# A cross-attention layer on one core: two passes over the scores in one software pipeline, straight code instead of loops

## The chip, the cores and the metric

One core of a Trainium2 chip. The time is device microseconds for one execution of the whole program. Engines: PE is TensorE, ACT ScalarE, DVE VectorE, POOL GpSimd, SP the queue that issues every DMA of this kernel.

## The reference

For B = 8 batches of S = 256 tokens, D = 1024 features, 32 heads of 32 features, all in f32:

```python
x = (hidden - mu) * rsqrt(var + 1e-5) * ln_gamma + ln_beta     # layer norm over 1024
Q = split_heads(x @ Wq.T)
K = V = split_heads(ctx)                                        # [8, 256, 1024]
scores = einsum('bhsd,bhtd->bhst', Q, K) / sqrt(32)             # masked with -inf
probs = softmax(scores)
attn = einsum('bhst,bhtd->bhsd', probs, V)
return hidden + merge_heads(attn) @ Wout.T
```

## The kernel before

**Numbers as pairs of f16.** Weights, normalised x, context, q and attention output are kept as a high and a low f16 part. A product takes three matmuls (`PASSES`). The high part is a copy by ACT, the low part (value minus high part) an operation of DVE; each such pair of operations on a 128x512 PSUM tile is a "fill" or "split" (`wq_split`, `wo_split`, `z_split`, `k_split`, `q_split`; z is the normalised x, transposed).

**Two passes over the scores.** Softmax needs the log of the sum of exponentials (lse) for each query row, and the probabilities are wanted with keys on partitions. So every batch has 16 steps of a first pass (`scores_s`, L399: four matmuls into a four-bank score buffer; `max_step`, L700: two maxima by DVE; `row_sums`, L554: four exps by ACT with an accumulated sum), and 16 steps of a second pass (`scores_t`, L426: four matmuls with the lse rows stacked in; `exp_step`, L572: one exp of 128x1024 by ACT; `probs_times_v`, L440, once for two steps; `att_split` by ACT and DVE). lse goes half a batch at a time: `ln_sums`, `exp_ln` on ACT, `lse_half` on DVE, two transposes on PE (`l_transposes`), `lse_rows` on DVE (five operations), three DMAs into row 97 to 99 of `q_stack`.

**Buffers.** Two score buffers `score[0]`, `score[1]` (four PSUM banks together of the eight, 2 banks each) are used alternately by both passes; `pv[0..1]` and `mm[0..1]` are one bank each. Step n waits for the reader of step n-2.

**Order of a batch.** `iteration(b)` writes the order of every engine by hand. First the 16 steps of the first pass of batch b, among which PE does the transposes of z and of the context of batch b+1 and the 96 output matmuls of batch b-1 (`o_matmuls`, L378); then the 16 steps of the second pass, among which it does nearly all 192 q matmuls of batch b+1 (`q_matmuls`, L354). DVE does row statistics, the Newton steps for 1/sqrt(var) and the normalising of batch b+2 in the second pass. POOL multiplies by gamma and adds beta, broadcast to all partitions, before the transposes (`scale_and_shift`, L284).

**Loops.** PE runs batches 1 to 6 in `pe.Fori(1, B - 1, 2)` (L514), two batches to a turn, three turns; ACT, DVE, SP and POOL have loops of their own (L628, L830, L262, L293).

**DMAs.** `fill_k_stack` and `fill_q_stack` copy the parts of k and q from 128 partitions to stacks of 32-partition groups: 12 DMAs each and a 13th for the mask, issued by SP in one order with all loads and stores (`iteration`, L190).

## Time and profile before

| | us |
|---|---|
| median of three runs | 649.28 |
| lowest, highest | 645.79, 653.34 |
| the profiled execution, in all | 647.76 |
| its span, first to last instruction | 646.0 |
| mean granted clock of TensorE, share of full | 0.976 |

How the profile is read: a row of the timeline has the start in us from the span's start, the length in us, the engine, the line of the kernel, the operation, what it writes and reads with its shape, the number of instructions merged into the row, and in brackets how long the engine sat idle before it and what ended the wait. "issue" there is a wait for nothing that the profile shows. Rows of groups give the count, total busy time and mean ns of one, and the idle time before them. The second number of a group of matmuls in the timeline includes a tail after the last, so that neighbouring groups overlap a little.

### The profile page before, as it was taken

The page shows a single profiled execution, that of the slowest core. Times are in us where ns is not written, and L with a number is a line of the kernel's source. Part 1 is how long each engine was busy: PE and PEld are TensorE (multiplying, and loading weights), DVE is VectorE, ACT ScalarE, POOL GpSimd, SP SyncE. Part 2 cuts the span into 40 slices and gives each one's busy share as a digit, 9 for nine tenths or more (in the row PEclk, how much of TensorE's full clock was granted, in tenths as well). Part 3 has the DMA queues.
Part 4 walks back from the last instruction along what each step waited for, and adds up shares of the span by engine and source line. Part 5 has one row for each costly group of instructions (what it writes and reads, how often), then busy time and mean ns, then how long its engine had stood idle before and what let it go on. Part 6 is the DMA issues. An engine that isn't in the chain of part 4 may idle for free.

```text
span 646.0 us, 13668 instructions
## 1 busy us (share of the span) xinstructions
PE 586.4 (91%) x4768; PEld 394.7 (61%) x4768; DVE 378.4 (59%) x813; ACT 457.5 (71%) x1377; POOL 80.8 (13%) x38
## 2 busy tenths in 40 slices
PE   3688688999999999689999999969999999998897
PEld 3587466656776577455776567635676558744443
DVE  6856686478545865258654876238763793168311
ACT  2633898798768976469767986639866996689850
POOL 2406000600060003200032000500015000000000
PEclk9999699999999999979999999969999999999999
DMA  8787122434344243413335162331523431422203
GB/s 329 273 211 195 43 70 66 116 115 116 106 117 128 82 117 106 133 29 90 108 110 136 53 164 64 91 114 50 149 63 91 133 110 36 117 50 66 69 2 98
DMA packets 37020, 69.67 MB, mean 108 GB/s; under 512 B 8833, under 2 KB 10081, under 8 KB 36962
## 3 DMA queue, kind: packets, MB, share of 16 engines
q1 hardware_dynamic: 36962, 68.84, 36.9%
q8 instruction: 44, 0.72, 0.5%
q14 instruction: 14, 0.11, 0.1%
HBM read 34.61 MB, written 8.39 MB: 67 GB/s over the span
## 4 chain that ended last, share of the span: by engine, by line
PE 65%; DVE 10%; ACT 10%; issue 6%; DMA 4%; SPq 4%; DVEq 0%
PE mm L369 20%; PE mm L394 17%; PE pv L448 10%; PE score L436 9%; ACT score L560 8%; PE score L412 6%; DVE nmax L706 4%; SPq L152 2%; PE pv L334 2%; DMA x_nat<-in_x 2%; DVE o_buf L748 1%; PE pv L349 1%; ACT probs L577 1%; SPq L171 1%; DMA probs<-in_L_xattn_Wq 1%
## 5 line engine op out<-in xcount | busy, mean ns | idle before, releaser
L560 ACT ACTIVATE score<-score,nmax 128x256 f32<-128x256 f32 x512 | 232.5, 475 | 16.0 <-DVE nmax L706 15.3
L706 DVE TENSOR_REDUCE nmax<-score 128x2 f32<-128x512 f32 x256 | 164.0, 685 | 66.3 <-PE score L412 65.8
L394 PE MATMUL mm<-woT,aT 128*128 128x512 f16 x768 | 186.6, 384 | 1.5 <-DVE o_buf L748 1.5
L369 PE MATMUL mm<-zT,wqT 128*128 128x256 f16 x1536 | 185.2, 274 | 2.0 <-DVE zT L657 2.0
L577 ACT ACTIVATE probs<-score 128x1024 f32<-128x1024 f32 x128 | 124.0, 1024 | 71.7 <-PE score L436 71.4
L369 PEld LDWEIGHTS mm<-zT,wqT 128*128 128x128 f16 x1536 | 150.1, 98 | 23.5 <-issue 2.9
L394 PEld LDWEIGHTS mm<-woT,aT 128*128 128x128 f16 x768 | 75.5, 98 | 74.8 <-DVE o_buf L748 4.4
L560 ACT ACTIVATION_READ_ACCUMULATOR score<-score,nmax 128x1 f32 x512 | 119.6, 234 | 0.0
L412 PE MATMUL score<-k_stack,q_stack 97*128 97x256 f16 x512 | 81.0, 281 | 31.0 <-issue 14.1
L287 POOL TENSOR_TENSOR x_nat<-x_nat,gamma_b 128x1024 f32<-128x1024 f32 x16 | 41.7, 2605 | 409.9 <-DVE x_nat L697 409.9
L741 DVE TENSOR_TENSOR aT<-pv,aT 128x256 f16<-128x256 f32 x64 | 27.0, 424 | 112.6 <-ACT aT L583 111.8
L412 PEld LDWEIGHTS score<-k_stack,q_stack 97*128 97x128 f16 x512 | 47.9, 100 | 68.7 <-ACT score L560 27.0
L436 PE MATMUL score<-q_stack,k_stack 100*128 100x256 f16 x512 | 67.8, 274 | 2.9 <-ACT probs L577 1.1
L448 PE MATMUL pv<-probs,ctx_sb 128*32 128x256 f32 x1024 | 68.5, 385 | 0.9 <-DVE aT L741 0.6
L436 PEld LDWEIGHTS score<-q_stack,k_stack 100*128 100x128 f16 x512 | 45.4, 98 | 29.7 <-issue 18.5
L448 PEld LDWEIGHTS pv<-probs,ctx_sb 128*32 128x32 f32 x1024 | 27.3, 109 | 25.5 <-issue 13.6
L546 ACT ACTIVATE zT<-pv 128x512 f16<-128x512 f32 x32 | 19.3, 605 | 27.8 <-PE pv L334 27.8
L289 POOL TENSOR_TENSOR x_nat<-x_nat,beta_b 128x1024 f32<-128x1024 f32 x16 | 38.8, 2424 | 1.3
L748 DVE SCALAR_TENSOR_TENSOR o_buf<-mm,res 128x512 f32<-128x512 f32 x32 | 21.8, 681 | 17.3 <-PE mm L394 17.3
L583 ACT ACTIVATE aT<-pv 128x256 f16<-128x256 f32 x64 | 24.9, 393 | 8.5 <-PE pv L448 8.5
L662 DVE SCALAR_TENSOR_TENSOR qT<-mm,qT 128x512 f16<-128x512 f32 x32 | 22.1, 690 | 14.6 <-ACT qT L552 14.1
L552 ACT ACTIVATE qT<-mm 128x512 f16<-128x512 f32 x32 | 19.6, 611 | 14.8 <-PE mm L369 14.8
(46 smaller groups left out, 322.7 us busy)
## 6 DMA issues: line engine op xcount, KB each, us to landing
k_stack<-kT SPq DMA_DIRECT2D x192, 64.0 KB, 2.0
q_stack<-qT SPq DMA_DIRECT2D x192, 64.0 KB, 2.4
x_nat<-in_x SPq DMA_DIRECT2D x8, 1024.0 KB, 5.3
ctx_sb<-in_ctx SPq DMA_DIRECT2D x8, 1024.0 KB, 6.3
res<-in_x SPq DMA_DIRECT2D x32, 256.0 KB, 3.5
out<-o_buf SPq DMA_DIRECT2D x32, 256.0 KB, 2.5
probs<-in_L_xattn_Wq SPq DMA_DIRECT2D x8, 512.0 KB, 7.3
probs<-in_L_xattn_Wout SPq DMA_DIRECT2D x8, 512.0 KB, 6.4
```

The lines of the kernel that those rows point to most:

```text
L287: pool.tensor_tensor(x_nat[:, st], x_nat[:, st], gamma_b[:], ALU.mult).then_inc(gamma_done, 1)
L289: pool.tensor_tensor(x_nat[:, st], x_nat[:, st], beta_b[:], ALU.add).then_inc(z_done, 1)
L369: last = pe.matmul(mm[i % 2][:, m2 * S:(m2 + 1) * S], wqT[:, wp, k, m * P:(m + 1) * P], zT[:, zp, k, :], start=(v2 == 0), stop=(v2 == KT * ...
L394: last = pe.matmul(mm[i % 2][:], aT[:, ap, k, st * P:(st + 1) * P], woT[:, wp, k, nh * 512:(nh + 1) * 512], start=(v == 0), stop=(v == O_M ...
L412: last = pe.matmul(score[n % 2][:, j, :], q_stack[0:S_ROWS, h, j, gl, st * P:(st + 1) * P], k_stack[0:S_ROWS, pb, h, j, gl, :], start=True ...
L436: last = pe.matmul(score[n % 2][:, j, :], k_stack[0:T_ROWS, pb, h, j, gl, tt * P:(tt + 1) * P], q_stack[0:T_ROWS, h, j, gl, :], start=True ...
L448: last = pe.matmul(pv[g % 2][DH * j:DH * (j + 1), 0, :], ctx_sb[:, pb, tt, g * P + DH * j:g * P + DH * (j + 1)], probs[:, g % 2, tt, j, :] ...
L560: last = act.activation(score[n % 2][:, j, :], score[n % 2][:, j, :], ACT.Exp, bias=nmax[:, st, h, j, gl:gl + 1], accum_out=sums[:, st, h, ...
L577: act.activation(probs[:, g % 2, tt], score[n % 2][:], ACT.Exp).then_inc(exp_done, 1)
L706: dve.tensor_reduce(nmax[:, st, h, at, gl], score[n % 2][:, at, :], AX.X, ALU.max, negate=True).then_inc(max_done, 1)
L741: dve.tensor_tensor(aT[:, 1, g, :], pv[g % 2][:, 0, :], aT[:, 0, g, :], ALU.subtract).then_inc(a_lo, 1)
L748: dve.scalar_tensor_tensor(out=o_buf[:, i % 2, :], in0=mm[i % 2][:], scalar=1.0 / W_SCALE, in1=res[:, i % 2, :], op0=ALU.mult, op1=ALU.add ...
```

## The change

The kernel is reordered as a whole.

- **One pipeline of slots.** Every engine runs `slot(b, t)` for t = 0 to 15. A slot has step t of the second pass of batch b, and the step of the first pass that lies 12 steps further on (`LEAD = 12`, `first_step`): of batch b for t < 4, of batch b+1 from t = 4. Twelve slots of "batch -1" with no second pass come first, and among them are the transposes and splits of Wout.
- **PSUM.** `score_s` for the first pass and `score_t` for the second, one each of two banks; one bank each for `pv`, `tr` (all transposes), `mo` (output) and `mq` (q). Where there were two buffers of a kind there is one.
- **Matmuls dealt out.** `Q_TAIL`, `Q_HEAD` and `O_AT` give each slot its q matmuls (12 or 16, none in two slots) and output matmuls (5, 6 or 9).
- **gamma and beta behind the transposes.** They are loaded as 16 rows of 128, transposed once, and applied by DVE per partition when it copies the transposed tile from PSUM to `t_f32` (`z_scale`, two operations; `k_scale`, one). POOL then makes the high and the low f16 part (`z_split`, `k_split`: a copy and a subtract of 128x512); for the first batch ACT makes the high part. ACT has no z and k copies afterwards.
- **Buffers in SBUF.** `q_stack` and `aT` double, `probs`, `qT`, `kT` half; the context is loaded twice, once for the transposes (`c_nat`) and in halves for the second product (`v_nat`). The residual is loaded into `o_buf` (a ring of three) and added in place.
- **`probs_times_v`** is called for each step, not for two.
- **The last batch's output** uses four PSUM banks, with no wait between its tiles.
- **Start.** Order of loads and of work changed: z of batch 0 first, q tiles between the transposes of Wq.
- **No loops.** Every engine's code is written out.

The core of the diff, the buffers and what a slot is dealt first:

```diff
-        score = [es.enter_context(nc.psum_tensor(f"score{i}", [P, J, S], F32)) for i in range(2)]
-        pv = [es.enter_context(nc.psum_tensor(f"pv{i}", [P, 2, S], F32)) for i in range(2)]
-        mm = [es.enter_context(nc.psum_tensor(f"mm{i}", [P, 512], F32)) for i in range(2)]
+        score_s = es.enter_context(nc.psum_tensor("score_s", [P, J, S], F32))
+        score_t = es.enter_context(nc.psum_tensor("score_t", [P, J, S], F32))
+        pv = es.enter_context(nc.psum_tensor("pv", [P, 2, S], F32))
+        tr = es.enter_context(nc.psum_tensor("tr", [P, 2, S], F32))
+        mo = es.enter_context(nc.psum_tensor("mo", [P, 2, S], F32))
+        mq = es.enter_context(nc.psum_tensor("mq", [P, 2, S], F32))
...
+Q_TAIL = [108 + 12 * min(t, 7) for t in range(STEPS + 1)]
+Q_HEAD = [0] * 10 + [16, 32, 48, 64, 80, 96, 108]
+O_AT = [0, 6, 12, 18, 24, 29, 34, 39, 48, 57, 62, 67, 72, 77, 82, 87, 96]
+Q_ENDS = {2: (1, 2), 6: (1, 3), 11: (2, 0), 14: (2, 1)}
```

PE's waits of the two passes, and its slot:

```diff
+            def scores_s(b, n):
...
-                if n >= 2:
-                    pe.wait_ge(sum_done, b * STEPS + n - 1)
+                    pe.wait_ge(sum_done, b * STEPS + n)
...
+            def scores_t(b, n):
...
-                    pe.wait_ge(exp_done, b * STEPS + n - 1)
+                if b or n:
+                    pe.wait_ge(exp_done, b * STEPS + n)
...
+            def slot(b, t):
+                s_b, s_n = first_step(b, t)
+                if b >= 0:
+                    scores_t(b, t)
+                if t and b >= 0:
+                    probs_times_v(b, t - 1)
+                elif b >= 1:
+                    probs_times_v(b - 1, STEPS - 1)
+                if b < 0:
+                    wo_transposes(WO_AT[t])
+                if t == 5 and b >= 0:
+                    l_transposes(b, 1, 8 * min(b + 2, B))
+                if b + 2 < B:
+                    if t == 6:
+                        k_transposes(b + 2, 0, 2 * b + 2)
+                    if t == 7:
+                        z_transposes(b + 2, 0, 2 * b + 2)
...
+                if b + 1 < B:
+                    q_matmuls(b + 1, Q_TAIL[t], Q_TAIL[t + 1])
+                if b + 2 < B:
+                    q_matmuls(b + 2, Q_HEAD[t], Q_HEAD[t + 1])
+                if s_b < B:
+                    scores_s(s_b, s_n)
...
+                if b >= 1:
+                    at = O_AT_LAST if b == B - 1 else O_AT
+                    o_matmuls(b - 1, at[t], at[t + 1])
```

ACT's slot:

```diff
+            def slot(b, t):
+                s_b, s_n = first_step(b, t)
+                if b < 0:
+                    wo_split(WO_AT[t])
+                else:
+                    exp_step(b, t)
+                if t and t % 2 == 0 and b >= 0:
+                    att_split(b, t // 2 - 1)
...
+                if t in Q_ENDS and b + Q_ENDS[t][0] < B:
+                    ahead, i = Q_ENDS[t]
+                    q_split(b + ahead, i)
+                if s_b < B:
+                    row_sums(s_b, s_n)
```

DVE's slot:

```diff
+            def slot(b, t):
...
+                if t in (4, 8, 12) and b >= 1:
+                    add_residual(b - 1, t // 4 - 1, mo[:])
...
+                    if t == 7:
+                        z_scale(b + 2, 0)
...
+                if t and t % 2 == 0 and b >= 0:
+                    att_split(b, t // 2 - 1)
...
+                if t == 5 and b >= 0:
+                    lse_rows(b, 1)
+                if t == 13 and b + 1 < B:
+                    lse_rows(b + 1, 0)
+                if 0 <= b < B - 2:
+                    if t < 2:
+                        row_stats(b + 2, t)
+                    if t == 2:
+                        row_var(b + 2)
+                    if t in (2, 3, 4):
+                        row_rstd(b + 2, t - 2)
+                    if t in (5, 6):
+                        normalise(b + 2, t - 5)
+                if s_b < B:
+                    max_step(s_b, s_n)
...
+                if t == 4 and b >= 0:
+                    lse_half(b, 1)
```

POOL's split of a fill, and how every engine runs through the slots:

```diff
+            def z_split(a, i):
+                f = z_fill(a, i)
+                pool.wait_ge(f32_done, f + 1)
+                if i == 0:
+                    pool.wait_ge(q_ready, a * TILES)
+                at = slice(2 * i, 2 * i + 2)
+                pool.tensor_copy(zT[:, 0, at], t_f32[:, f % 2]).then_inc(split_hi, 1)
+                pool.wait_ge(split_hi, z_split_at(a, i))
+                pool.tensor_tensor(zT[:, 1, at], t_f32[:, f % 2], zT[:, 0, at], ALU.subtract).then_inc(split_done, 1)
...
+            for b in range(-1, B):
+                for t in range(PRE if b < 0 else 0, STEPS):
+                    slot(b, t)
```

## Rows read from the trace of the kernel before

**Rows 1.** Page, busy time, share of the span and instructions of each engine.

```profile
PE 586.4 (91%) x4768; PEld 394.7 (61%) x4768; DVE 378.4 (59%) x813; ACT 457.5 (71%) x1377; POOL 80.8 (13%) x38
```

**Rows 2.** Timeline of PE: where batches begin, the loop's return, the last matmuls.

```profile
64.04 0.60 PE L412 MATMUL score<-k_stack,q_stack 97*128 97x256 f16 x4 [1.69 <-DMA q_stack<-qT]
...
128.99 0.61 PE L412 MATMUL score<-k_stack,q_stack 97*128 97x256 f16 x4
...
198.89 0.61 PE L412 MATMUL score<-k_stack,q_stack 97*128 97x256 f16 x4
...
267.79 1.07 PE L448 MATMUL pv<-probs,ctx_sb 128*32 128x256 f32 x16
...
276.25 0.82 PE L412 MATMUL score<-k_stack,q_stack 97*128 97x256 f16 x3 [4.03 <-issue]
...
568.59 0.61 PE L412 MATMUL score<-k_stack,q_stack 97*128 97x256 f16 x4
...
625.08 17.66 PE L394 MATMUL mm<-woT,aT 128*128 128x512 f16 x81
```

**Rows 3.** Timeline of PE: groups of one kind in a row.

```profile
58.49 2.78 PE L369 MATMUL mm<-zT,wqT 128*128 128x256 f16 x24
61.25 1.09 PE L317 MATMUL pv<-ident,probs 128*128 128x128 f32 x8
...
107.50 1.07 PE L448 MATMUL pv<-probs,ctx_sb 128*32 128x256 f32 x16
108.50 1.05 PE L436 MATMUL score<-q_stack,k_stack 100*128 100x256 f16 x8
```

**Rows 4.** Timeline: scores to maximum, maximum to row sums, the last of four.

```profile
90.50 0.61 PE L412 MATMUL score<-k_stack,q_stack 97*128 97x256 f16 x4 [0.94 <-ACT score L560]
...
91.15 1.29 DVE L706 TENSOR_REDUCE nmax<-score 128x2 f32<-128x512 f32 x2
...
225.26 1.28 DVE L706 TENSOR_REDUCE nmax<-score 128x2 f32<-128x512 f32 x2
...
225.98 0.45 ACT L560 ACTIVATE score<-score,nmax 128x256 f32<-128x256 f32 x1 [0.36 <-DVE nmax L706]
...
227.71 0.21 ACT L560 ACTIVATION_READ_ACCUMULATOR score<-score,nmax 128x1 f32 x1
```

**Rows 5.** Groups by line: att copy, att split and row statistics (busy, mean ns).

```profile
L583 ACT ACTIVATE aT<-pv 128x256 f16<-128x256 f32 x64 | 24.9, 393 | 8.5 <-PE pv L448 8.5
L741 DVE TENSOR_TENSOR aT<-pv,aT 128x256 f16<-128x256 f32 x64 | 27.0, 424 | 112.6 <-ACT aT L583 111.8
L669 DVE BATCH_NORM_STATS2 stats<-x_nat 128x6 f32<-128x512 f32 x32 | 19.7, 670 | 6.6 <-DMA x_nat<-in_x 6.6
```

**Rows 6.** Timeline of ACT and DVE: exps, Wout's fills, the first layer norm.

```profile
8.32 0.28 DVE L676 BATCH_NORM_AGGREGATE mean_var<-stats 128x2 f32<-128x12 f32 x2
...
11.63 1.53 DVE L697 TENSOR_SCALAR x_nat<-x_nat,mean_var,rstd 128x1024 f32<-128x1024 f32 x2
...
33.79 1.09 ACT L533 ACTIVATE woT<-pv 128x512 f16<-128x512 f32 x2 [2.46 <-PE pv L317]
34.42 1.29 DVE L646 SCALAR_TENSOR_TENSOR woT<-pv,woT 128x512 f16<-128x512 f32 x2 [2.37 <-ACT woT L533]
...
103.77 3.76 ACT L577 ACTIVATE probs<-score 128x1024 f32<-128x1024 f32 x4
```

**Rows 7.** Timeline: five operations of the lse rows to their DMAs; twelve DMAs of q.

```profile
104.99 0.41 DVE L729 TENSOR_SCALAR l_rows<-pv 16x256 f16<-16x256 f32 x1 [0.39 <-PE pv L423]
...
106.94 1.64 SPq L177 DMA_DIRECT2D q_stack<-l_rows  x2
...
119.95 7.49 SPq L171 DMA_DIRECT2D q_stack<-qT  x12
```

**Rows 8.** One line's instructions: POOL's add of beta, min/median/max ns.

```profile
L289 POOL TENSOR_TENSOR x_nat<-x_nat,beta_b x16: 2352/2358/3422, 15.5 to 490.4; 128x1024 f32<-128x1024 f32 x16
```

**Rows 9.** Page, DMA issues: count, KB each, median us to landing.

```profile
q_stack<-qT SPq DMA_DIRECT2D x192, 64.0 KB, 2.4
```

More of the change, by code:

```diff
@@ L387, in o_matmuls @@
[L387 to L395 removed]
+                        pe.wait_ge(a_lo, c * G + G - 1)
@@ L430, in scores_t @@
                     pe.wait_ge(l_in[h], (b + 1) * L_ROWS * DMA)
-                if n < 2:
-                    pe.wait_ge(sum_done, b * STEPS + STEPS - 1 + n)
-                else:
-                    pe.wait_ge(exp_done, b * STEPS + n - 1)
+                if b or n:
+                    pe.wait_ge(exp_done, b * STEPS + n)
                 for j in range(J):
-                    last = pe.matmul(score[n % 2][:, j, :], k_stack[0:T_ROWS, pb, h, j, gl, tt * P:(tt + 1) * P], q_stack[0:T_ROWS, h, j, gl, :],
+                    last = pe.matmul(score_t[:, j, :], k_stack[0:T_ROWS, b % 2, h, j, gl, tt * P:(tt + 1) * P], q_stack[0:T_ROWS, b % 2, h, j, gl, :],
@@ new lines, in probs_times_v @@
+            def probs_times_v(b, n):
+                g, tt = n // 2, n % 2
+                h, gl = divmod(g, HALF)
+                pe.wait_ge(exp_done, b * STEPS + n + 1)
+                if n in (0, STEPS // 2):
+                    pe.wait_ge(v_in[h], (b + 1) * DMA)
+                if b == 0 and n == 0:
+                    pe.wait_ge(wo_lo, W_FILLS)
+                elif tt == 0:
+                    pe.wait_ge(a_lo, b * G + g)
+                for j in range(J):
+                    at = gl * P + DH * j
+                    last = pe.matmul(pv[DH * j:DH * (j + 1), 0, :], v_nat[:, h, tt, at:at + DH], probs[:, n % 2, j, :],
+                                     start=(tt == 0), stop=(tt == ST - 1), skip_group_check=True)
+                last.then_inc(pv_done, 1)
@@ new lines, in _ @@
+            for f in range(4):
+                wq_split(f)
+            for i in range(TILES):
+                act.wait_ge(f32_done, i + 1)
+                act.activation(zT[:, 0, 2 * i:2 * i + 2], t_f32[:, i % 2], ACT.Copy).then_inc(z0_hi, 1)
+            for f in range(4, 8):
+                wq_split(f)
+            q_split(0, 0)
+            for f in range(8, 12):
+                wq_split(f)
+            q_split(0, 1)
+            for f in range(12, 16):
+                wq_split(f)
+            q_split(0, 2)
@@ L632, in _ @@
+            for b in range(-1, B):
+                for t in range(PRE if b < 0 else 0, STEPS):
+                    slot(b, t)
+            att_split(B - 1, G - 1)
         @block.vector
@@ L655, in z_split, with z_scale @@
-            def z_split(a, i):
-                dve.wait_ge(z_hi, a * FILLS + i + 1)
-                dve.tensor_tensor(zT[:, 1, 2 * i:2 * i + 2, :], pv[i % 2][:], zT[:, 0, 2 * i:2 * i + 2, :], ALU.subtract).then_inc(z_lo, 1)
+            def z_scale(a, i):
+                f = z_fill(a, i)
+                dve.wait_ge(fill_ready, f + 1)
+                if a == 0 and i >= 2:
+                    dve.wait_ge(z0_lo, i - 1)
+                elif a:
+                    dve.wait_ge(split_done, f - TILES - 1)
+                for m in range(2):
+                    k = 2 * i + m
+                    last = dve.tensor_scalar(t_f32[:, f % 2, m, :], tr[:, m, :], gb[:, 0, k:k + 1], gb[:, 1, k:k + 1], ALU.mult, ALU.add)
+                last.then_inc(f32_done, 1)
@@ L830, in _ @@
[L830 to L835 removed]
+            layer_norm(0)
+            dve.wait_ge(gb_ready, 1)
+            dve.tensor_copy(gb[:].rearrange("p a k -> p (a k)"), tr[:, 0, 0:2 * KT]).then_inc(gb_done, 1)
+            dve.wait_ge(gb_done, 1)
+            for i in range(TILES):
+                z_scale(0, i)
@@ new lines, in _ @@
+            for f in range(8):
+                wq_split(f)
+            dve.wait_ge(mask_in, DMA)
+            dve.tensor_scalar(mask_st, mask_u8, -1.0, 3e38, ALU.add, ALU.mult).then_inc(mask_ok, 1)
+            q_split(0, 0)
+            for f in range(8, 12):
+                wq_split(f)
+            q_split(0, 1)
+            for f in range(12, 16):
+                wq_split(f)
+            k_scale(0, 0)
+            k_scale(0, 1)
+            q_split(0, 2)
+            k_scale(0, 2)
+            k_scale(0, 3)
@@ L839 @@
+            layer_norm(1)
+            for b in range(-1, B):
+                for t in range(PRE if b < 0 else 0, STEPS):
+                    slot(b, t)
+            add_residual(B - 2, 3, mo[:])
+            att_split(B - 1, G - 1)
+            for i in range(TILES):
+                add_residual(B - 1, i, o_bank_last[i])
 _INS = ["x", "ctx_4096", "mask_BxS2_bf1", "L0_xattn_Wq", "L0_xattn_Wout", "L0_xattn_ln_gamma", "L0_xattn_ln_beta"]
```

891 lines of the change are left out of this document (399 added, 492 removed).

## The prediction

> **What bounds the kernel now.** I read the page's busy line first: PE is busy 91% of the span, ACT 71%, DVE 59%, POOL 13% [rows 1]. PE is the engine to follow, so I read its timeline for where one batch begins. Batch 1 starts its first-pass scores at 128.99, batch 2 at 198.89: 69.90 us. Batch 7 starts at 568.59, so six batches took 439.60, where six of 69.90 would be 419.40. The missing 20.2 us stand in one kind of place [rows 2]: after 267.79 (last product of batch 2, about 1.0 long) PE issues nothing useful until 276.25, with "issue" as releaser, and it is the return of `pe.Fori`. The clock is then down for some microseconds. There are two returns, 10.1 us each. The entry at 128.99 and the exit at 568.59 show no such gap.
>
> The pitches of PE's work [rows 3], from one row's start to the next's or, where another follows, less the tail of 0.17 by which a group's busy time overlaps the next: a q matmul 0.115 (24 in 61.25 - 58.49 = 2.76), a transpose 0.115 (8 in 1.09 - 0.17), a pv record 0.0625 (16 in 1.00), a score matmul 0.11 (8 in 1.05 - 0.17), and an output matmul 0.216 (81 in 17.66 - 0.17 [rows 2]). A batch has 192 q (22.1), 96 output (20.7), 64 + 64 scores (14.1), 128 pv records (8.0), 36 transposes (4.1): 69.0 us. So outside the loop's return the kernel before is within 1 us of PE's own work. **The change cannot gain more than about 1 us in a steady batch**; its possible gains are the 20.2 of the loop, batch 0 (65 us from 64.04 to 128.99 [rows 2], with about 49 of work) and the start.
>
> The Trainium skill (Runtime: NRT & Kernel Launch, section Instruction fetch mechanics) says that prefetch is sequential and a taken branch to code outside the window makes the engine wait for a fetch; the rows of the return agree, and straight code would by that rule give these microseconds back.
>
> **The new chain.** The change moves nothing off PE (the same matmuls and transposes, plus one small transpose). What it changes is who waits. Before, both passes alternate over two score buffers. After, the first pass has one buffer `score_s`, the second one `score_t`, and a slot does on ACT: exp of the second pass, att copy (even slots), a q copy (four slots), then the row sums of the first pass. On DVE the att split and other work stand ahead of `max_step`. The scores of slot t+1 may only start when the row sums of slot t are done. The price of that loop [rows 4]: scores start to max start 0.65 (90.50 to 91.15), max start to first row-sum exp 0.72 (225.26 to 225.98), four row sums to the end of the last accumulator read 1.94 (225.98 to 227.71 + 0.2), and 0.05 to PE. That is **3.36 us**, for odd slots with nothing else. In an even slot ACT must first do exp 0.94 (four in 3.76 [rows 6]) and the att copy 0.39, then DVE the att split 0.425, all of it ahead of the max [rows 5]: 0.94 + 0.39 + 0.05 + 0.425 + 0.05 + 0.72 + 1.94 = **4.51 us**. PE's mean slot is 69.0 / 16 = 4.3 us. A pair of slots is 7.9 by the chain and 8.6 by PE, so the bare pipeline is bound by PE with 0.7 to spare in a pair. But DVE's work for batch b+2 is put into the same slots ahead of the max:
>
> - t=0: two bn_stats, 1.3 [rows 5]. Slot 5.8.
> - t=2: variance and first Newton round. The 17 small instructions run 3.31 in all [rows 6], 9 of them 1.7. Slot 6.2.
> - t=4: Newton, 0.8. Slot 5.3.
> - t=5: `lse_half` ends after the max of slot 4, its transpose follows, then `lse_rows` 1.95 [rows 7] and a normalise of 0.77 [rows 6], then the max. Slot 5.1.
> - t=6: normalise again, 0.77. Slot 5.3.
> - t=7, 8: scaling of the transposed x, 0.84 a pair from PSUM by the att split's row, twice in each slot. Its splits are on POOL.
>
> **POOL.** The trace has no POOL copy and no 512-column subtract. A two-input add of 1024 columns takes 2.35 to 3.42, median 2.36 [rows 8], so 512 columns are 1.2; the copy lies between nothing and that 1.2. A fill then costs 1.2 to 2.4, and 3.4 if it runs like the slowest row; I take 2.1, because the copy has one input but its own start. Six fills come in slots 6 to 8, through one bank `tr`, two buffers `t_f32` and DVE's order; the chain k0, k1, z0..z3 ends about 10 us after the row sums of slot 6, and the q matmuls of slot 9 wait for it. They would otherwise start about 7.5 us after. So **2 to 3 us** of stall.
>
> The Trainium skill (GPSIMD Engine Reference, section 4.1) advises VectorE for elementwise work and gives two-input operations on GPSIMD as about 2x slower. No row here compares the two on one shape. By its figure of 2.6 cycles for an element a 512-column subtract would be 1.1 us; the sum would hardly move by that.
>
> Walking slot by slot, each the later of PE and chain, lateness carried on: stalls of 1.0 (t=0 to 1), 1.5 (2 to 3), 1.4 (4 to 5, with the wait of the lse transpose), 1.5 (6, 7), 2 (9), 0.3 (q bank, single, freed by ACT and DVE 2.7 after the last matmul while PE comes back after 2.2). A steady batch becomes 69 + 7 to 8 = **76 us**, against 69.9.
>
> **The sum.**
> - Start to first scores: norm is done at 13.2 [rows 6]; four z fills at 2.2 (transpose, scale, ACT copy, POOL subtract) to 22; q tiles 0 and 1 (5.5 each) with the wq fills between, whose DVE splits are serial behind them, to 39.4; k scale to 41.5; two POOL fills to 44. Only then SP issues the 13 DMAs of k_stack, and the 12 of q_stack behind them in its queue, at 0.625 each (12 in 7.49 [rows 7]): 15.6, and 2.4 to land [rows 9]. First scores at **62**, against 64.04, with q tile 3 and all but a fill of the wo transposes still to do.
> - Twelve leading slots: ACT wo copy 0.55 and DVE wo split 0.64 (pairs in 1.09 and 1.29 [rows 6]) stand ahead of each max: 4.0 a slot; two to a slot, the fills of batch 1 and lse bring **56**.
> - Batch 0, no output matmuls, by the chain: eight even and eight odd slots 63, DVE's extras and POOL 9: **72**.
> - Batches 1 to 5: 5 x 76 = **380**. Batch 6, no fills, chain 63 + 2: **65**. Batch 7: four slots of 3.9, twelve of 2.4 on PE: **45**.
> - Tail: 0.5 + 96 x 0.216 = 20.7 and 3.3 from PE's end to the last store (625.08 + 17.66 = 642.74 of 646.0 [rows 2]): **24.5**.
> Sum 704.5 on the span. The profiled run before is 646.0 on the span and 647.76 in all; the median is 649.28, so add 2 to 3. Some of the steps overlap at the joints (fills that slip into batch 0's idle PE), 5 us off: I forecast **702 us**, 8% slower. Where the 20.2 of the loop go: they are gained on PE and spent in the chain's stalls (5 x 7, batch 0, the leading slots).
>
> Code fetched in a straight line is costed at nothing: hidden by work queued ahead on each engine; if it stalled as at the return, each time would be 3 to 4 us.
>
> **Rivals.**
> - *Extras hide* (13%): the steady batch is near 71, because DVE's extras fall before the att copy arrives, which is so in odd slots, but in even slots only if the att split is late anyway. 25 us less, and the leading slots at 3.6: about 670.
> - *PE stays the bound everywhere* (10%, the other side): one mechanism, the chain between two first-pass scores stays under PE's slot of 4.3, also with extras. Then the loop's 20.2 and much of batch 0's 16 come back: 62 + 44 + 52 + 5 x 69 + 55 + 42 + 24.5 = 625. It decides if extras ahead of the max cost less than 0.9 in a slot; the rows give 0.8 to 2.7. ACT and DVE shares under 75% speak for it, being averages.
> - *A tie* (6%): both at half strength, 643 to 655.
> - *POOL is the bound of the fills* (8%): at 3.4 a fill and more, six are 20 us against 13 of PE's slots, 5 us more in each of 7 batches: 740.
> - *Forecast* (63%): 680 to 735.
>
> By these cases, with 1% being what a measurement here can tell from no change: faster 10%, same 6%, slower 84%. The range takes the first rival and most of the tie at its low end and leaves the last one out: 652 to 735.
>
> **What would show it.** The starts of first-pass scores 16 slots apart in the middle of the run: near 76 (forecast), 69 to 71 (rivals). PE idle ahead of score_s released by ACT's row sums, near 30 us or more in all; ACT idle released by the max. POOL's copy at 0.4 to 1.2. The gap of type "issue" gone, and no clock dip with it. First scores near 62, the first second-pass scores near 118. It would be wrong if even slots in batch 0 take under 4 us, or PE is over 95% busy in the middle.

## The result, and the profile after

| | before | after |
|---|---|---|
| median of the runs | 650.74 | 723.95 |
| lowest, highest | 645.79, 653.34 | 723.57, 724.90 |
| span of the profiled execution | 646.0 | 723.1 |
| PE, ACT, DVE, POOL busy | 586.4, 457.5, 378.4, 80.8 | 620.3, 427.4, 387.8, 111.1 |
| granted clock, share of full | 0.976 | 0.948 |

The change makes the kernel slower by a factor of 1.114 (95% interval 1.107 to 1.121). The forecast was 702, 8% slower, with a range of 652 to 735: the measured time is inside the range, 22 us above the forecast.

The page of the kernel after, engines' line first, then slices of a fortieth of the span. They answer to [rows 1]: PE is busy 34 us longer, part of it at a lower granted clock, and its share fell.

```profile
PE 620.3 (86%) x4769; PEld 393.6 (54%) x4769; DVE 387.8 (54%) x830; ACT 427.4 (59%) x1317; POOL 111.1 (15%) x130
...
PE   3873677777989899999999999989998999877998
...
PEclk8795979987899999999999999999999999999999
```

What the reader is to see: the low digits are at the left, in the start, in the leading slots and in batch 0. From slice 11 on PE is nearly full, but for slices 35 to 37 (8, 7, 7), which are batch 6 and the start of batch 7; and a steady batch is still 6.1 us longer than before.

The timeline of PE in one steady batch, batch 3, its first four slots and slot 4's start. It answers to [rows 2]: a batch begins with its first second-pass scores (L490).

```profile
361.76 0.60 PE L490 MATMUL score_t<-q_stack,k_stack 100*128 100x256 f16 x4
362.30 0.64 PE L506 MATMUL pv<-probs,v_nat 128*32 128x256 f32 x8
362.87 1.48 PE L427 MATMUL mq<-zT,wqT 128*128 128x256 f16 x12
364.19 0.60 PE L478 MATMUL score_s<-k_stack,q_stack 97*128 97x256 f16 x4
364.63 1.46 PE L435 MATMUL mo<-woT,aT 128*128 128x512 f16 x6
365.92 0.60 PE L490 MATMUL score_t<-q_stack,k_stack 100*128 100x256 f16 x4
...
374.77 0.64 PE L506 MATMUL pv<-probs,v_nat 128*32 128x256 f32 x8
376.73 1.48 PE L427 MATMUL mq<-zT,wqT 128*128 128x256 f16 x12 [1.32 <-DVE qT L719]
...
379.79 0.60 PE L490 MATMUL score_t<-q_stack,k_stack 100*128 100x256 f16 x4
...
437.76 0.60 PE L490 MATMUL score_t<-q_stack,k_stack 100*128 100x256 f16 x4
```

The batch lasts 437.76 - 361.76 = 76.00 us; so do batches 2, 4 and 5, while batch 1 takes 77.7. Four score matmuls and eight pv records take 1.11 (361.76 to 362.87); 8 and 16 took 1.88 before [rows 3], so two such slots now take 0.34 more.

Busy time of each engine by stage (us; then PE, PEld, DVE, ACT, POOL, granted clock, DMA share, GB/s): the start, the leading slots, batch 0, batch 3, batch 6.

```profile
0.00:72.50 72.50, 40.73 (x270) 34.39 (x271) 31.67 (x75) 14.82 (x25) 12.33 (x18) 0.76 0.54 171
72.50:131.90 59.40, 41.36 (x276) 31.37 (x274) 37.23 (x70) 30.39 (x108) 14.13 (x16) 0.84 0.38 113
131.90:208.00 76.10, 61.66 (x478) 40.25 (x475) 42.37 (x94) 50.13 (x159) 14.15 (x16) 0.86 0.28 80
...
361.80:437.80 76.00, 71.55 (x582) 45.66 (x581) 45.47 (x99) 50.85 (x161) 14.10 (x16) 1.00 0.38 113
...
589.80:654.00 64.20, 55.82 (x441) 31.50 (x440) 31.43 (x62) 49.38 (x159) 0.00 (x0) 1.00 0.29 83
```

And the waits of PE in batch 3, longest in all first (us, times, longest):

```profile
PE mq L427 <- DVE qT L719: 1.3, 1, 1.3
PE tr L389 <- DVE t_f L704: 1.0, 2, 0.7
PE tr L389 <- issue: 0.8, 1, 0.8
PE mq L427 <- POOL zT L331: 0.7, 1, 0.7
PE tr L409 <- DVE lse L775: 0.4, 1, 0.4
```

Together 4.2 us of idle time in waits that are named; in all PE is not busy for 4.4 of the 76.00. Before, it was busy 68.86 of 69.90. So of the 6.1 us by which the batch is longer, 3.4 are more idle time and 2.7 are PE's own (71.55 against 68.86).

The stages against the sum of the prediction, in us:

| stage | forecast | measured |
|---|---|---|
| to the first first-pass scores | 62 | 72.5 |
| leading slots | 56 | 59.4 |
| batch 0 | 72 | 76.1 |
| batches 1 to 5 | 380 | 381.7 |
| batch 6 | 65 | 64.2 |
| batch 7 | 45 | 44.0 |
| tail | 24.5 | 25.1 |
| span | 704.5 | 723.1 |

### The profile page after: what moved, and what is told of

It is laid out like the page before. It is cut to its first block, busy times and chain, and to the rows that moved or that the text cites. A ratio compares the mean times of both kernels' runs of the same rounds, so it can differ in the third digit from the quotient of the medians.

```text
span 723.1 us, 12971 instructions
## 1 busy us (share of the span) xinstructions
PE 620.3 (86%) x4769; PEld 393.6 (54%) x4769; DVE 387.8 (54%) x830; ACT 427.4 (59%) x1317; POOL 111.1 (15%) x130
## 4 chain that ended last, share of the span: by engine, by line
PE 55%; DVE 20%; ACT 14%; issue 5%; POOL 2%; SPq 2%; DMA 1%; DVEq 0%; ACTq 0%
PE mq L427 19%; PE mo L435 13%; ACT score_s L613 9%; DVE nmax L762 7%; PE pv L506 6%; PE score_s L478 5%; PE score_t L490 4%; DVE t_f L704 3%; ACT probs L630 3%; PE tr L389 2%; PE tr L400 2%; DVE aT L798 2%; PE score_s L435 1%; POOL zT L331 1%; SPq L208 1%
## 5 line engine op out<-in xcount | busy, mean ns | idle before, releaser
L613 ACT ACTIVATE score_s<-score_s,nmax 128x256 f32<-128x256 f32 x512 | 228.3, 446 | 191.5 <-DVE nmax L762 191.5
L427 PE MATMUL mq<-zT,wqT 128*128 128x256 f16 x1536 | 197.8, 284 | 22.2 <-DVE qT L719 13.7
L762 DVE TENSOR_REDUCE nmax<-score_s 128x2 f32<-128x512 f32 x256 | 164.4, 684 | 96.0 <-PE score_s L478 95.2
L427 PEld LDWEIGHTS mq<-zT,wqT 128*128 128x128 f16 x1536 | 150.9, 102 | 69.9 <-DVE qT L719 20.2
L435 PE MATMUL mo<-woT,aT 128*128 128x512 f16 x696 | 169.1, 379 | 0.2 <-DVE o_buf L805 0.2
L630 ACT ACTIVATE probs<-score_t 128x1024 f32<-128x1024 f32 x128 | 132.2, 1033 | 17.0 <-PE score_t L490 16.9
L613 ACT ACTIVATION_READ_ACCUMULATOR score_s<-score_s,nmax 128x1 f32 x512 | 103.8, 203 | 0.0
L478 PE MATMUL score_s<-k_stack,q_stack 97*128 97x256 f16 x512 | 81.2, 283 | 14.7 <-ACT score_s L613 13.9
L341 POOL CAST kT<-t_f 128x512 f16<-128x512 f32 x32 | 19.6, 611 | 426.2 <-DVE t_f L714 410.4
L506 PE MATMUL pv<-probs,v_nat 128*32 128x256 f32 x1024 | 82.3, 393 | 1.2 <-DVE aT L798 1.2
L490 PE MATMUL score_t<-q_stack,k_stack 100*128 100x256 f16 x512 | 78.9, 277 | 1.4 <-ACT probs L630 1.4
L490 PEld LDWEIGHTS score_t<-q_stack,k_stack 100*128 100x128 f16 x512 | 50.1, 99 | 34.2 <-ACT probs L630 3.7
L389 PE MATMUL tr<-ident,x_nat 128*128 128x128 f32 x128 | 24.8, 326 | 19.9 <-DVE t_f L704 11.7
L605 ACT ACTIVATE qT<-mq 128x512 f16<-128x512 f32 x32 | 19.6, 613 | 37.3 <-DMA q_stack<-qT 22.8
L704 DVE TENSOR_SCALAR t_f<-tr,gb 128x256 f32<-128x256 f32 x64 | 31.7, 537 | 12.4 <-PE tr L389 10.5
L400 PE MATMUL tr<-ident,c_nat 128*128 128x128 f32 x128 | 21.3, 291 | 19.4 <-DVE t_f L714 19.4
```

What stands on the lines that cost most here:

```text
L389: last = pe.transpose(tr[:, n // 2, st * P:(st + 1) * P], x_nat[:, st, k * P:(k + 1) * P], ident[:])
L427: last = pe.matmul(mq[:, m2, :], wqT[:, wp, k, m * P:(m + 1) * P], zT[:, zp, k, :], start=(v2 == 0), stop=(v2 == KT * 3 - 1))
L435: return pe.matmul(bank, aT[:, c % 2, ap, k, st * P:(st + 1) * P], woT[:, wp, k, nh * 512:(nh + 1) * 512], start=(v == 0), stop=(v == O_MM ...
L478: last = pe.matmul(score_s[:, j, :], q_stack[0:S_ROWS, b % 2, h, j, gl, st * P:(st + 1) * P], k_stack[0:S_ROWS, b % 2, h, j, gl, :], start ...
L490: last = pe.matmul(score_t[:, j, :], k_stack[0:T_ROWS, b % 2, h, j, gl, tt * P:(tt + 1) * P], q_stack[0:T_ROWS, b % 2, h, j, gl, :], start ...
L506: last = pe.matmul(pv[DH * j:DH * (j + 1), 0, :], v_nat[:, h, tt, at:at + DH], probs[:, n % 2, j, :], start=(tt == 0), stop=(tt == ST - 1) ...
```

## The experiments

Where each version spends its span. "Steady" is a batch in the middle, "batch 7 on" reaches to the end. The versions of the kernel before have no leading slots; their stages begin with first-pass scores. In the kernel before itself a return of the loop falls behind the first score matmul of batches 3 and 5 and splits its cost between two batches: batches 1 to 6 take 69.9, 72.9, 76.9, 72.8, 77.2, 69.9. In the pipelined versions batch 1 is not steady (77.7 in the changed kernel), so that a row with five steady batches adds up to slightly less than the span.

| version | first scores | leading | batch 0 | steady | batch 6 | batch 7 on | span |
|---|---|---|---|---|---|---|---|
| before | 64.0 | | 64.9 | 69.9, and 72.9 + 76.9 about a return | 69.9 | 77.4 | 646.0 |
| e1, PE's loop written out | 66.0 | | 64.6 | 69.90 | 69.9 | 77.4 | 627.4 |
| e2, all loops written out | 67.2 | | 65.4 | 69.90 | 69.9 | 77.3 | 629.4 |
| e3, one score buffer | 68.5 | | 85.5 | 86.87 | 86.9 | 98.7 | 773.9 |
| e4, finer dealing | 66.2 | | 68.5 | 72.41 | 71.6 | 81.9 | 650.3 |
| after | 72.5 | 59.4 | 76.1 | 76.00 | 64.2 | 69.1 | 723.1 |
| e5, q DMAs first | 58.6 | 61.6 | 73.3 | 76.01 | 64.3 | 69.1 | 708.6 |
| e6, extras last | 71.7 | 61.6 | 69.4 | 73.23 | 64.3 | 69.1 | 702.8 |
| e7, POOL short | 72.8 | 59.4 | 72.3 | 75.18 | 64.2 | 69.1 | 715.4 |
| e8, e5 and e6 | 60.2 | 62.9 | 69.4 | 73.23 | 64.2 | 69.1 | 692.5 |
| e9, att split late | 58.2 | 61.9 | 67.7 | 74.93 | 62.9 | 67.5 | 693.4 |
| e10, Wout's split late | 59.3 | 62.6 | 67.7 | 74.93 | 62.9 | 67.6 | 695.2 |
| e11, e10 and halves | 58.3 | 58.8 | 63.1 | 73.77 | 58.7 | 65.8 | 673.7 |
| e12, e8 and halves | 58.6 | 60.5 | 65.9 | 73.23 | 62.4 | 67.7 | 681.4 |

### The loop alone

Theory: the 20.2 us at the loop's returns [rows 2] are gained by straight code alone; the pipeline loses them elsewhere. Rival: they belong to the joint of batches.

```diff
-            with pe.Fori(1, B - 1, 2) as b:
+            for b in range(1, B - 1, 2):
```

> The kernel before with only PE's loop written out (three turns of two batches in straight code); the other engines keep their loops. Theory (the 20.2 us at the loop's two returns are the fetch of code and nothing else): the two gaps at 267.79 and its like vanish, batches 1 to 6 take 69.9 us each, 646.0 - 20.2 = 626 us on the span, 628 in all. Rival (the gap is the joint of two batches, or the whole stream fetched anew is as slow): no change, 646.

Measured 630.16 against 649.76, ratio 0.970 (0.968 to 0.972). The kernel before idles twice at its first return, with one score matmul between: 2.96 us, and then the 4.03 of [rows 2] (timeline of PE, before):

```profile
271.82 0.39 PE L412 MATMUL score<-k_stack,q_stack 97*128 97x256 f16 x1 [2.96 <-issue]
```

The same place now (timeline of PE, e1):

```profile
269.42 1.07 PE L448 MATMUL pv<-probs,ctx_sb 128*32 128x256 f32 x16
270.42 0.61 PE L412 MATMUL score<-k_stack,q_stack 97*128 97x256 f16 x4
```

There is no gap, and all six batches take 69.90. So it is the loop's return that costs the time, and not the joint of two batches. What in the return takes it, the fetch of code or something else, no run separates. Busy time in batch 1 of e1 (columns as above):

```profile
130.60:200.50 69.90, 68.86 (x584) 46.97 (x580) 44.16 (x98) 54.97 (x168) 9.91 (x4) 1.00 0.37 108
```

PE is busy 68.86 of 69.90: the two-phase order left 1 us in a batch, as the prediction said.

> The kernel before with all five loops written out. Theory (ACT, DVE, SP and POOL are never late at their own returns, since they wait for PE there): the same as with PE's alone, 626 us on the span, within 2. Rival (their returns cost too, hidden behind PE's so far, up to one 3 us wait per batch in the six turns of ACT or DVE): 615 to 623 us.

Measured 631.26, ratio 0.971 (0.970 to 0.973): the other engines' loops cost nothing that can be measured. **e1 beats both kernels**, and it takes from the change nothing but PE's loop written out.

### One score buffer

The kernel before with straight code, and one number in a wait changed:

```diff
                 if n >= 2:
-                    pe.wait_ge(sum_done, b * STEPS + n - 1)
+                    pe.wait_ge(sum_done, b * STEPS + n)
```

> All loops written out, and first-pass scores wait for the row sums of the step just before, not of the one before that, as if there were one score buffer; nothing else. Theory (the chain scores, max, four row sums has a period of 3.36 us): the first pass takes 16 x 3.4 and some 0.35 in each of the eight steps in which ACT also copies a fill, 57 us, in place of 39.4 (198.89 to 238.31 before); 17 more in each of eight batches: 626 + 136 = 760 us. Rival (PE has enough other work to hide the single buffer): under 640 us.

Measured 775.67 (one run) where 760 was forecast. A steady batch takes 86.87, 16.97 more than with two buffers; 17 were forecast. Batch 0 and the stretch from batch 7 on lose more than that, 20.1 and 21.4 (against e2). Timeline of PE, e3, a step with a fill and one without:

```profile
246.82 0.61 PE L412 MATMUL score<-k_stack,q_stack 97*128 97x256 f16 x4 [1.00 <-ACT score L560]
...
250.38 0.61 PE L412 MATMUL score<-k_stack,q_stack 97*128 97x256 f16 x4 [1.00 <-ACT score L560]
...
340.80 0.61 PE L412 MATMUL score<-k_stack,q_stack 97*128 97x256 f16 x4 [1.00 <-ACT score L560]
...
344.16 0.61 PE L412 MATMUL score<-k_stack,q_stack 97*128 97x256 f16 x4 [1.24 <-ACT score L560]
```

The step with a fill is 3.56 (246.82 to 250.38), of which PE stands 1.00. The step without one is 3.36 (340.80 to 344.16), of which it stands 1.24. So the chain of one buffer is real, with exactly the price that the prediction gave it. In the changed kernel it hides behind a slot of 4.3 us of PE's work as long as nothing is put into it.

### Finer dealing

The kernel before with straight code; in the second pass 4 scores, 8 q, 8 pv, again and again, in place of 8, 16, 16.

```diff
                 for g in range(G):
                     scores_t(b, pb, 2 * g)
-                    scores_t(b, pb, 2 * g + 1)
+                    if g == 0:
+                        scores_t(b, pb, 1)
                     if not last:
-                        q_matmuls(b + 1, q_at[g], q_at[g + 1], c)
+                        q_matmuls(b + 1, q_at[g], (q_at[g] + q_at[g + 1]) // 2, c)
...
-                        probs_times_v(b, pb, g - 1)
+                        probs_times_v(b, pb, g - 1, (0,))
+                        scores_t(b, pb, 2 * g + 1)
+                    if not last:
+                        q_matmuls(b + 1, (q_at[g] + q_at[g + 1]) // 2, q_at[g + 1], c)
+                    if g >= 1:
+                        probs_times_v(b, pb, g - 1, (1,))
```

> All loops written out, and in the second pass PE's work is dealt as finely as after the change: per step 4 score matmuls, 8 q, 8 pv records, instead of 8, 16, 16 for two steps. Theory (turning between kinds of matmuls costs PE: after the change 4 scores and 8 pv records take 0.53 + 0.57 = 1.10 us against 1.88 for 8 and 16 before, 2.6 us in a batch): a batch goes from 69.9 to 72.5, in all 626 + 8 x 2.6 = 647 us. Rival (the pitch after the change is due to waits on ACT and DVE): 626 us.

Measured 652.11 (one run; 647 was forecast), a steady batch 72.41, 2.51 more for the same matmuls. Timeline of PE, e4:

```profile
251.36 0.61 PE L436 MATMUL score<-q_stack,k_stack 100*128 100x256 f16 x4
251.81 1.04 PE L369 MATMUL mm<-zT,wqT 128*128 128x256 f16 x8
252.77 0.64 PE L450 MATMUL pv<-probs,ctx_sb 128*32 128x256 f32 x8
253.34 0.61 PE L436 MATMUL score<-q_stack,k_stack 100*128 100x256 f16 x4
```

Eight pv records take 0.57 where sixteen took 1.00, and eight q matmuls 0.96 where sixteen took 1.85 (179.58 to 181.43 in the trace before), with no wait in the rows. Two steps of the second pass take 3.97 (251.36 to 255.33) where they took 3.73 (177.70 to 181.43 before), so each of the three more turns between groups costs PE some 0.08.

Not all of the 2.51 is that. Busy time and one wait of PE in a steady batch of e4:

```profile
207.12:279.53 72.41, 70.64 (x585) 45.67 (x581) 44.26 (x98) 55.56 (x168) 9.88 (x4) 1.00 0.35 104
PE pv L450 <- DVE aT L750: 0.7, 1, 0.7
```

PE is busy 70.64 against 68.86 in e1, 1.8 more; the other 0.7 is a wait for a pv bank that the coarse order did not have. In the changed kernel PE is busy 71.55, 2.7 more than in e1. Turns are what the prediction did not have; e4 shows 1.8 of the 2.7, and the other 0.9 has no run of its own (the changed kernel also deals the first pass, the output matmuls and the transposes among the slots).

### The start

The swap, in SP's queue:

```diff
-            fill_k_stack(0, 0)
             fill_q_stack(0, 0)
+            fill_k_stack(0, 0)
```

> The changed kernel with one swap in SP's queue at the start: the 12 DMAs of q_stack(0, 0) ahead of the 13 of k_stack(0, 0). Theory (PE's 14.9 us of idle time at 51 to 66 come from ACT, which waits 22.8 us for those q DMAs before it may overwrite the half-size qT, with DVE and the transposes behind it): q DMAs are issued from about 40.5, the copy of q tile 2 is free at 51, k DMAs end at 58, first scores start at 58 to 60 in place of 72.5, in all 724 - 13 = 711 us. Rival (k_stack's own lateness sets the start): first scores near 72, no change.

The timeline of the changed kernel, which made the theory:

```profile
50.72 0.60 PE L400 MATMUL tr<-ident,c_nat 128*128 128x128 f32 x4
54.62 0.59 SPq L209 DMA_DIRECT2D k_stack<-k_stack  x1
55.25 7.55 SPq L218 DMA_DIRECT2D q_stack<-qT  x12
64.27 0.60 ACT L605 ACTIVATE qT<-mq 128x512 f16<-128x512 f32 x1 [22.76 <-DMA q_stack<-qT]
64.90 0.69 DVE L719 SCALAR_TENSOR_TENSOR qT<-mq,qT 128x512 f16<-128x512 f32 x1 [20.19 <-ACT qT L605]
65.51 0.68 DVE L714 TENSOR_SCALAR t_f<-tr 128x512 f32<-128x512 f32 x1
66.25 1.11 PE L400 MATMUL tr<-ident,c_nat 128*128 128x128 f32 x4 [14.92 <-DVE t_f L714]
```

Read it from the bottom: PE waits 14.92 for DVE's scaled tile, DVE stands 20.19 behind a q copy of ACT, ACT 22.76 for DMAs of q_stack, and SP issues those only at 55.25, behind thirteen DMAs of k_stack. `qT` is half as large as before; tile 2 overwrites tile 0. With the swap (e5):

```profile
52.75 0.66 PE L400 MATMUL tr<-ident,c_nat 128*128 128x128 f32 x4 [1.57 <-DVE t_f L714]
...
58.57 0.61 PE L478 MATMUL score_s<-k_stack,q_stack 97*128 97x256 f16 x4 [2.11 <-DMA k_stack<-k_stack]
```

First scores are 13.9 us earlier in the profiled execution, in all 713.90 (ratio to before 1.099, 1.094 to 1.104). That is 10.1 less than the change between medians; its four runs lie between 710.4 and 718.8, so this gain is known to a few us only. What the first scores wait for now is k_stack's landing.

### DVE's extras

```diff
-                if 0 <= b < B - 2:
-                    if t < 2:
-                        row_stats(b + 2, t)
-                    if t == 2:
-                        row_var(b + 2)
-                    if t in (2, 3, 4):
-                        row_rstd(b + 2, t - 2)
-                    if t in (5, 6):
-                        normalise(b + 2, t - 5)
                 if s_b < B:
                     max_step(s_b, s_n)
...
                     q_split(b + ahead, i)
+                if 0 <= b < B - 2:
+                    if t < 2:
+                        row_stats(b + 2, t)
+                    if t == 2:
+                        row_var(b + 2)
+                        row_rstd(b + 2, 0)
+                    if t == 3:
+                        row_rstd(b + 2, 1)
+                        row_rstd(b + 2, 2)
+                    if t in (4, 5):
+                        normalise(b + 2, t - 4)
```

> The changed kernel with DVE's row statistics, variance, Newton rounds and normalising of batch b+2 moved from ahead of the max of their slot to the slot's end (Newton's third round and the two normalisings one slot earlier). Theory (they lengthen the chain max, row sums, next scores; a steady batch has 1.32 us of idle time at the q bank in slot 3 and 0.43 at the lse transpose for it, batch 0 has much more): a steady batch goes from 76.0 to about 74, batch 0 from 76.1 to about 69, in all 724 - 5 x 2 - 7 = 707 us. Rival (PE's own work of 71.5 and POOL's fills set the batch, the extras fall into gaps anyway): 722 to 725 us.

Measured 703.03 (ratio to before 1.080, 1.077 to 1.082), 20.9 less than the change. A steady batch 73.23 (2.8 less), batch 0 69.4 (6.7 less; PE's busy time in it fell too, from 61.7 to 56.6 for the same matmuls, with the granted clock at 0.94 in place of 0.86, so part of the 6.7 goes with the clock). All of PE's waits in a steady batch of e6:

```profile
PE tr L389 <- DVE t_f L704: 1.3, 2, 0.7
PE mq L427 <- POOL zT L331: 0.7, 1, 0.7
```

The 1.32 at the q bank, the 0.8 of "issue" (a wait for the normalised x, by what the move removed) and the 0.4 at the lse transpose are gone. The extras were in the chain, as the prediction had it; their sum over a steady batch is 2.8, where the prediction's walk gave the slots with extras 1.0 + 1.5 + 1.4 + 1.5 = 5.4.

### POOL

POOL's copies and subtracts on 32 of 256 columns for batches 1 to 7; most of the f16 parts of z and k are then not computed. The edit of z's copy; its subtract, and both of k, are cut in the same way:

```diff
-                pool.tensor_copy(zT[:, 0, at], t_f32[:, f % 2]).then_inc(split_hi, 1)
+                pool.tensor_copy(zT[:, 0, at, 0:32], t_f32[:, f % 2, :, 0:32]).then_inc(split_hi, 1)
```

> The changed kernel with POOL's copies and subtracts cut to 32 of 256 columns in each half, for batches 1 to 7, so that most of z's and k's parts are not made (this part of the computation is left out). Theory (POOL bounds the fills of slots 6 to 9): PE's idle time of 0.83 + 0.38 + 0.65 + 0.74 us there goes nearly to zero, a steady batch 73.5 to 74, in all about 710. Rival (the single bank tr and DVE's order set it, POOL only the 0.74 ahead of the q matmuls of slot 9): a steady batch at 75.3, in all about 718.

A steady batch 75.18 (0.8 less), batch 0 72.3 (3.8 less), in all 717.18 (one run). The rival is right for the steady batch: POOL sets only the wait ahead of slot 9's q matmuls. The waits for `t_f` stay, which are the one bank `tr` filled by PE and emptied by DVE in turn. In batch 0, where PE has no output matmuls to do meanwhile, POOL costs more (why was not tested). The operations themselves, line by line, min/median/max ns (changed kernel):

```profile
L341 POOL CAST kT<-t_f x32: 611/611/613, 43.3 to 573.7; 128x512 f16<-128x512 f32 x32
L343 POOL TENSOR_TENSOR kT<-t_f,kT x32: 1152/1157/1163, 44.0 to 574.4; 128x512 f16<-128x512 f32 x32
```

### Both together

> The changed kernel with both the swap in SP's queue and DVE's extras at the slot's end. Theory: the two gains are in different stretches and add up: 724 - 13 - 17 = 694 us. Rival (one hides behind the other): no better than the better of the two, 707 or 711.

Measured 692.52 (ratio 1.063, 1.061 to 1.066): 31.4 less than the change, where 10.1 and 20.9 add up to 31.0. They are in different stretches and add, as far as the spread of e5 lets one see.

### The att split: a miss

```diff
-                if t and t % 2 == 0 and b >= 0:
-                    att_split(b, t // 2 - 1)
...
                 if s_b < B:
                     max_step(s_b, s_n)
+                if t and t % 2 == 0 and b >= 0:
+                    att_split(b, t // 2 - 1)
```

> As with both the swap in SP's queue and DVE's extras at the slot's end, and DVE's att split put behind the max of its slot. Theory (an even slot costs 4.51 because exp, att copy and att split stand ahead of the max; with the max first, only exp and att copy, 1.33, stand beside scores and max, 1.37): even slots 3.4 like odd ones where PE is not the bound. Batch 0 from 69.4 to 61.5, batch 6 from 64.2 to about 57, four slots of batch 7 by 2, a steady batch by 0.5: 692.5 - 20 = 673 us. Rival (those stretches are set by PE and by POOL's fills): less than 4 us gained, 689 or more.

Measured 695.41 (ratio 1.068, 1.062 to 1.073): no gain on 692.52. Batch 0 gained 1.7, not 8; a steady batch lost 1.7, of which 1.1 are four waits of PE for the att split ahead of its pv matmuls. Timeline of batch 0, e9:

```profile
131.68 0.41 DVE L798 TENSOR_TENSOR aT<-pv,aT 128x256 f16<-128x256 f32 x1
...
132.25 0.64 PE L506 MATMUL pv<-probs,v_nat 128*32 128x256 f32 x8 [0.89 <-DVE aT L798]
...
132.82 1.49 PE L427 MATMUL mq<-zT,wqT 128*128 128x256 f16 x12
...
134.14 0.60 PE L478 MATMUL score_s<-k_stack,q_stack 97*128 97x256 f16 x4
```

The att split also frees the one bank `pv`. PE stops at its pv matmuls for it, and q matmuls and the next first-pass scores are queued behind. The stall moved from DVE's queue to PE's. And the even slot was never 4.51. Batch 0 of e8, slot 4:

```profile
140.70 1.03 ACT L630 ACTIVATE probs<-score_t 128x1024 f32<-128x1024 f32 x1
...
143.09 0.45 ACT L613 ACTIVATE score_s<-score_s,nmax 128x256 f32<-128x256 f32 x1 [0.71 <-DVE nmax L762]
...
144.91 1.03 ACT L630 ACTIVATE probs<-score_t 128x1024 f32<-128x1024 f32 x1
```

From exp to exp it is 4.21. Adding up durations overstated it, as an engine starts the next operation before the last one's recorded end (the max starts at 142.38, the att split at 142.04 with a length of 0.43).

> The same, and in the twelve leading slots DVE's split of Wout's fill too stands behind the max. Theory (it lengthens the chain by 0.64 in each of twelve slots): leading slots from 62.9 to about 55, in all 7 to 8 us below the run with the att split moved, 665. Rival (the leading slots are slow by the clock, granted at 0.79 in them, and by POOL): 671 or more.

Edit: `wo_split` behind `max_step` in the same way. Measured 696.66 (ratio 1.070, 1.064 to 1.075), leading slots 62.6 against 61.9: no gain. The split likewise frees a Wout bank: in the leading slots PE waits 7.1 + 3.3 us for it in e10, 5.9 in e9. The rival's clock is not the cause either: it was granted at 0.87 in these slots of e10 and at 0.79 in those of e9.

### Handing the buffer over by halves

On top of e10, ACT signals after two of four row sums. (`score_s` is two banks of two heads each; the description of the kernel before calls one such buffer "four-bank", which is both buffers together.)

```diff
-                    pe.wait_ge(sum_done, b * STEPS + n)
+                    pe.wait_ge(half_done, b * STEPS + n)
                 for j in range(J):
+                    if j == 2 and b * STEPS + n:
+                        last.then_inc(s_ready, 1)
+                        pe.wait_ge(sum_done, b * STEPS + n)
...
+                    if j == 1:
+                        last.then_inc(half_done, 1)
...
-                dve.wait_ge(s_ready, b * STEPS + n + 1)
                 for j2 in range(2):
+                    dve.wait_ge(s_ready, 2 * (b * STEPS + n) + j2 + 1)
```

> The same, and the one first-pass score buffer is handed over by halves: ACT signals after two of four row sums, PE then writes the first two heads' scores while ACT reads the other two, DVE takes its first max at once. Theory (the chain max, row sums, scores goes from 3.36 to about 2.4 a slot, so batch 0 comes near PE's own 50 to 52): batch 0 from 61.5 to 53, leading slots to 46, batch 6 by 2: about 645 us; a steady batch stays at 72 to 73, being PE's. Rival (PE's queue, in order, stops at the second half's wait and gains nothing): within 3 us of the run before it.

Measured 678.75 (ratio 1.042, 1.037 to 1.048): 17.9 less than e10. Where the chain binds it is shorter: batch 0 by 4.6, batch 6 by 4.2, leading slots by 3.8; a steady batch by 1.2. The forecast of 645 stood on 665 for e10, which had measured 696.66; the step itself was forecast at 20 us and gave 17.9. It came from other places than said: the leading slots and batch 0 gave about half of the forecast (3.8 and 4.6 for 9 and 8.5), batch 6 and the steady batches more. In batch 0 PE is busy 52.1 of 63.1 in this run, so the chain still binds.

> The changed kernel with the swap in SP's queue, DVE's extras at the slot's end and the first-pass buffer handed over by halves, while the att split and Wout's splits stay ahead of the max as in the change. Theory (handing over by halves shortens the chain wherever it binds; putting the att split late only held up the pv matmuls through their one bank, and cost 1.7 us in a steady batch): a steady batch 73 or a little less, leading slots 59, batch 0 about 65, batch 6 about 60, in all 671 us, 7 below the run with both. Rival (both moves are needed together, halves only help where the max comes first): 688 or more.

Measured 684.06 (ratio 1.051, 1.048 to 1.054), between the two hypotheses. Against e8, which has the same order without halves, handing over by halves takes 3.5 us from batch 0, 2.4 from the leading slots, 1.8 from batch 6, 1.4 from batch 7 on and nothing from a steady batch, which is 73.23 in both; 8.5 in all between medians. So halves help by themselves where the chain binds, and the rival is wrong.

Against e11 it shows what the late splits do once the halves are there: a steady batch is 0.5 shorter without them (73.23 for 73.77; without halves it was 1.7), but the leading slots are 1.7 longer, batch 0 2.9 (65.9 for 63.1), batch 6 3.7 (62.4 for 58.7) and batch 7 on 1.9. In these runs a late split gains in batches 0, 6 and 7, where PE has less work, and loses in a steady batch. (The 1.7 of the leading slots says little: with one and the same code in them they took 59.4 to 62.9, in the change, e5, e6 and e8.)

## Why the prediction was right, and where its steps were not

- **PE's bound before, and the loop** (right). 20.2 us forecast, 18.6 on the span, 19.6 between medians (e1). Straight code costs nothing seen: the gaps of type "issue" ahead of first-pass scores are gone. The reading that PE issues nothing useful until 276.25 was short by one score matmul, at 271.82.
- **"The change cannot gain more than about 1 us in a steady batch"** (right): PE busy 68.86 of 69.90 (e1).
- **The chain of one buffer, 3.36 us** (right): e3 gave 3.36 in a step without a fill, and 16.97 of 17 in a batch. In batch 0 of e8 the first two slots, which have no att split, take 3.36 each (exps at 125.86, 129.22 and 132.58).
- **The even slot, 4.51** (mis-sized): 4.2. The place was right, and it is tied to a second chain through the bank `pv` that the prediction did not name (e9).
- **Steady batch, 69 + 7 to 8 = 76** (right sum, two wrong terms): PE's work is 71.5, 2.5 more than its 69.0, of which the finer dealing of the second pass is 1.8 (e4); the stalls are 4.4, not 7 to 8. By name: 1.32 at the q bank in slot 3 (forecast 0.3, and there 1.5 by the extras), 0.4 at the lse transpose, 1.0 + 0.8 in slots 7 and 8, 0.7 for POOL in slot 9 (forecast 2). That the sum came out at 76.00 is luck: the two errors cancel.
- **POOL's fill 2.1 us** (mis-sized): 0.61 + 1.16 = 1.77, inside the bounds 1.2 to 2.4 set from [rows 8]. The Trainium skill (GPSIMD Engine Reference, section 3.1) gives about 2.6 cycles for an element of a two-input operation, by estimate some 1.1 us for the subtract; the trace's 1.157 agrees.
- **"First scores at 62"** (wrong, the largest miss): 72.5. The working followed k_stack and q_stack through SP's queue, but gave q tile 2 no wait. It had one, for the q DMAs, since `qT` is half as large. 14.9 us of PE's idle time hang on it, and e5 takes 13.9 back.
- **Leading slots and batch 0** (both short): 3.4 and 4.1 over. The leading slots' 3.4 stay open. The clock was granted at 0.84 in them, but it does not explain them: they took 61.6 at 0.79 (e6), and 62.6 at 0.87 (e10). In batch 0 the prediction gave DVE's extras and POOL 9 together; without the extras it is 6.7 shorter (e6), without most of POOL's work 3.8 (e7), 10.5 if the two add, which no run tested.
- **"PE idle ahead of score_s released by ACT's row sums, near 30 us or more in all"** (wrong): 13.9 in all. Most of PE's idle time stands ahead of other work: it waits 13.7 for DVE's q splits, 11.7 and 19.4 for its scaled tiles (14.9 of it the start), 7.1 for lse. Neither sign of being wrong came: the even slot in batch 0 is 4.2 and not under 4 (e8), and PE is busy 94% of a steady batch, not over 95%.
- **"Some of the steps overlap at the joints, 5 us off"** (wrong): no row stood behind it, and the leading slots and batch 0, where it was to be found, came out longer than the sum had them. Without it and with the start's 10.5 the forecast would have been 717 on 724.

The forecast lies within the range, but its errors in the stages nearly all go one way: the start, the leading slots, batch 0 and the 5 us taken off add up to 23, of the 22 by which it was low; the others cancel to within 1.

Of the 95.7 us by which the change is longer than e1, batches 1 to 5 hold 32 (381.7 against 349.5). The other 63 are the filling of the pipeline, before batch 1 begins (208.1 against 130.6), less what batches 6 and 7 give back for the work done ahead (133.4 against 147.3). This is a count by stages: no run changed `LEAD`, so how much of the 63 a shorter lead would give back is not shown. What the runs did take back of the changed kernel's time is 45 us in all (e11, 678.75 for 723.95), and it is still slower than before.

## What to carry to other kernels

Before two phases are merged, look at how full the bound engine is inside each: where it is at 98%, as here, even dealing has nothing to fill, while what it costs stays (fewer buffers, more turns between kinds of work, a filling of the pipeline before the first batch). A single buffer passed round three engines is a chain: list everything that stands in each engine's queue ahead of the link, and then ask what else the moved operation frees. And when a buffer is halved, find who overwrites the other half, and which queue its release stands in, at the start above all, where no earlier batch covers it.
